# Preparing the experts' first weights in halves of 512 columns, with GpSimd's share behind each head's scaling

## What is computed

```python
x = x + attn_a(layernorm(x))   # 16 heads of 64, causal with ALiBi slopes, then w_out and b_out
x = x + ffn(layernorm(x))      # RMS norm times norm_w, gate, top 2 of 8 experts, swiglu
x = x + attn_b(layernorm(x))   # 8 heads of 128, rotary, causal
x = x + ffn(layernorm(x))      # the same weights again

t1 = jnp.einsum('td,efd->tef', flat, mlp1_w) + mlp1_b     # first weights of the experts: W1
act = _swiglu(t1, LIMIT)
y = jnp.einsum('tei,edi->ted', act, mlp2_w) + mlp2_b
```

## Time and profile before

| what | value |
|---|---|
| timed runs, median of 3 | 2192.08 us (2187.16 to 2192.74) |
| span of the profiled execution, which is also all of its own time that the profile gives | 2234.9 us |
| TensorE busy | 2095.9 us, 94% |
| VectorE busy | 1526.6 us, 68% |
| ScalarE busy | 1439.4 us, 64% |
| GpSimd busy | 1306.3 us, 58% |
| granted TensorE clock, mean | 0.984 |

### The profile page before, as it was taken

One profiled execution on the slowest core, in us unless ns is written; L12 is line 12 of the kernel. 1 busy time (PEld: TensorE's weight loads), 2 busy tenths in 40 slices (PEclk: granted clock), 3 DMA queues, 4 the chain that ended last, 5 costly groups with the idle time before them and its releaser, 6 DMA issues.

```text
span 2234.9 us, 38037 instructions
## 1 busy us (share of the span) xinstructions
PE 2095.9 (94%) x11450; PEld 1670.2 (75%) x11450; DVE 1526.6 (68%) x4368; ACT 1439.4 (64%) x3738; POOL 1306.3 (58%) x1458
## 2 busy tenths in 40 slices
PE   7899999999999999798998999999999999888995
PEld 6677777777777777576776788888888888676774
DVE  7868686868686868466666767566675765656567
ACT  5768686868686867443444777667676676734344
POOL 4655464646464655556665546667576665556663
PEclk9999999999999999999999999999999999999998
DMA  4320010101000000523241001001010000523246
GB/s 146 135 107 29 1 30 1 30 1 30 1 30 1 20 1 22 170 92 83 100 164 56 31 18 38 24 26 41 18 39 18 13 20 26 199 70 106 96 143 232
DMA packets 59500, 134.44 MB, mean 60 GB/s; under 512 B 12900, under 2 KB 30852, under 8 KB 58280
## 3 DMA queue, kind: packets, MB, share of 16 engines
q1 hardware_dynamic: 41576, 94.69, 12.3%
q0 software_dynamic: 17728, 37.32, 5.8%
HBM read 83.60 MB, written 48.40 MB: 59 GB/s over the span
## 4 chain that ended last, share of the span: by engine, by line
PE 75%; DVE 7%; ACT 6%; issue 5%; another core or an unknown queue 3%; DMA 2%; POOL 2%; SPq 0%; ACTq 0%; DVEq 0%; POOLq 0%
PE bank L650 5%; PE bank L1533 5%; PE bank L1553 5%; PE bank L2245 5%; PE bank L672 5%; PE bank L632 4%; PE bank L617 3%; PE bank L2218 3%; PE bank L1518 3%; PE bank L1433 3%; PE bank L618 3%; PE bank L1435 2%; PE bank L1434 2%; PE bank L2220 2%
## 5 line engine op out<-in xcount | busy, mean ns | idle before, releaser
L1157 POOL TENSOR_TENSOR P<-P,rc 128x128 f32<-128x128 f32 (+3 forms) x512 | 354.6, 724 | 351.1 <-DVE rc L964 350.9
L956 DVE CUSTOM_DVE_ANT_0 P<-bank,tab 128x512 f32<-128x512 f32 (+3 forms) x512 | 240.8, 486 | 111.1 <-PE bank L618 107.7
L794 ACT ACTIVATE P<-P,mn 128x128 f32<-128x128 f32 (+3 forms) x512 | 281.6, 552 | 31.1 <-DVE mn L956 26.7
L805 ACT COPY PT<-bank 128x512 f32<-128x512 f32 (+1 forms) x384 | 194.3, 516 | 105.2 <-PE bank L632 95.7
L1992 POOL TENSOR_TENSOR rf<-rp 128x512 f32<-128x512 f32 x128 | 163.7, 1279 | 138.4 <-DVE rp L1833 135.9
L1999 POOL TENSOR_TENSOR q<-rf,q 128x512 fp32r<-128x512 f32 x128 | 162.8, 1293 | 130.9 <-ACT q L1649 130.5
L2493 POOL DMA_INDIRECT yD<-Yf,place x142 | 144.3, 1016 | 148.5 <-ACT Yf L2316 122.2
L632 PE MATMUL bank<-cst,P 128*128 128x128 f32 x1280 | 207.2, 277 | 15.5 <-POOL P L1157 9.7
L617 PE MATMUL bank<-q 128*128 128x512 f32 (+3 forms) x512 | 185.0, 372 | 16.9 <-DVE mn L956 10.8
L632 PEld LDWEIGHTS bank<-cst,P 128*128 128x128 f32 x1280 | 153.1, 141 | 43.7 <-POOL P L1157 13.2
L324 POOL DMA_INDIRECT Gf<-hD,idx x142 | 147.1, 1036 | 59.3 <-issue 38.3
(11 more groups left out here) (257 smaller groups left out, 5913.7 us busy)
## 6 DMA issues: line engine op xcount, KB each, us to landing
hD<-hh SPq DMA_DIRECT2D x16, 512.0 KB
yg<-yD SPq DMA_DIRECT2D x14, 512.0 KB, 4.2
X<-in_x SPq DMA_DIRECT2D x8, 512.0 KB, 4.3
stage<-in_w SPq DMA_DIRECT2D x8, 512.0 KB, 3.5
w1hD<-W1A SPq DMA_DIRECT2D x8, 512.0 KB
w1lD<-stage SPq DMA_DIRECT2D x8, 512.0 KB
rD<-xn SPq DMA_DIRECT2D x8, 512.0 KB
W1lf<-w1lD SPq DMA_DIRECT2D x1, 4096.0 KB
```

What stands on the lines that cost most here:

```text
L794: i = e.activation(ps, ps, ACT.Exp, bias=mn[:, pb, t:t + 1], scale=-1.0, accum_out=rs[:, pb, t:t + 1])
L805: e.copy(PT[:, h % 2, PTO[cs[0]]:PTO[cs[0]] + w], bank[4 + n % 2][:, 0:w]).then_inc(q.a_pt, 1)
L956: e.tensor_tensor_reduce(out=P[:, pb, OFF[t]:OFF[t] + w], in0=score(h, t), in1=tab[:, 512 - w:512], scale=-SLOPES[h % 16], scalar=3e38, op ...
L1157: i = e.tensor_tensor(ps, ps, rc[:, h % 3, t:t + 1].broadcast_to([128, w]), ALU.mult)
```

## The change

W1 is prepared in 16 halves j = 2i + kc of 512 columns. Each half has its own place (stage[:, kc]) and its own semaphores d_w1s[kc] and d_w1o[kc]; the row w0 of expert i goes into one of two places of share, by i % 2. VectorE does norm_w1(u, 0) in the first half of unit u and norm_w1(u, 1) in the second. GpSimd does split_w1(2u-1) between scale(2u+1) and scale(2u+2), and split_w1(2u) at the end of unit u; the last half falls into unit 8. SyncE issues the first two loads together and afterwards load_w1(j+1) behind the stores of half j; stores are 256 KB. The diff, without the declaration of the semaphores:

```diff
@@ -817,7 +818,8 @@
                         if kc == 0 and bt:
                             e.wait_ge(q.m_lg, bt)
                         if kc == 0 and bt == 0:
-                            e.wait_ge(d_w1o, 32 * E)
+                            for s in d_w1o:
+                                e.wait_ge(s, 32 * E)
                         e.copy(hT[:, kc], bank[7][:]).then_inc(q.a_hT, 1)
                     def ratio(bt):
@@ -989,8 +991,9 @@
                                         ALU.subtract).then_inc(v_gw, 1)
                     def norm_w1(i, kc):
-                        e.wait_ge(d_w1s, 32 * i + 32)
-                        e.scalar_tensor_tensor(stage[:, kc], stage[:, kc], nw[:, kc:kc + 1], share[:, 0:512], ALU.mult,
+                        e.wait_ge(d_w1s[kc], (32, 16)[kc] * (i + 1))
+                        w0 = share[:, 512 * (i % 2):512 * (i % 2) + 512]
+                        e.scalar_tensor_tensor(stage[:, kc], stage[:, kc], nw[:, kc:kc + 1], w0, ALU.mult,
                                                ALU.subtract).then_inc(v_w1, 1)
@@ -1102,9 +1105,8 @@
                                 low(u + 2, hl)
                                 if hl:
                                     copy_k(u + 2)
-                            if bt == 0 and hl:
-                                norm_w1(p, 0)
-                                norm_w1(p, 1)
+                            if bt == 0:
+                                norm_w1(p, hl)
                             if v_tile(bt, p, hl):
                                 v_copy(*v_tile(bt, p, hl))
                             if p == 0 and bt:
@@ -1140,12 +1142,12 @@
                                         ALU.mult).then_inc(p_qs, 1)
-                    def split_w1(i):
-                        k = W1_ORDER[i]
-                        raw, H = stage[:].rearrange("p a b -> p (a b)"), W1h[:, k % W1_STAY]
-                        e.wait_ge(v_w1, 2 * i + 2)
+                    def split_w1(j):
+                        i, kc = divmod(j, 2)
+                        raw, H = stage[:, kc], W1h[:, W1_ORDER[i] % W1_STAY, 512 * kc:512 * kc + 512]
+                        e.wait_ge(v_w1, j + 1)
                         e.tensor_copy(H, raw).then_inc(p_w1, 1)
-                        e.wait_ge(p_w1, 2 * i + 1)
+                        e.wait_ge(p_w1, 2 * j + 1)
                         e.tensor_tensor(raw.bitcast(F32R), raw, H.bitcast(F32), ALU.subtract).then_inc(p_w1, 1)
@@ -1193,6 +1195,8 @@
                     for u in range(NU):
                         bt, p = divmod(u, 8)
                         scale(2 * u + 1)
+                        if 0 < u <= E:
+                            split_w1(2 * u - 1)
                         if u == NU - 1:
                             for a in range(4):
                                 gather(e, 0, q, a)
@@ -1210,7 +1214,7 @@
                         if 1 < p < 6 and bt + 1 < NB:
                             add_bias(bt + 1, p - 2)
                         if bt == 0:
-                            split_w1(u)
+                            split_w1(2 * u)
                         if p == 7 and bt and bt + 1 < NB:
                             for n in range(4 if bt == K1 else 2):
@@ -1275,23 +1279,35 @@
                             fetch_x(bt + 2)
                         if bt == 0:
                             e.wait_ge(d_b1, 48)
-                            for i, k in enumerate(W1_ORDER):
+                            def load_w1(j):
+                                i, kc = divmod(j, 2)
                                 if i:
-                                    e.wait_ge(d_w1o, 32 * i)
-                                e.dma_start(stage[:].rearrange("p a b -> p (a b)"), T["w1"][:, k]).then_inc(d_w1s, 16)
-                                e.dma_start(share[:, 0:512], w0D[k].partition_broadcast(128)).then_inc(d_w1s, 16)
-                                e.wait_ge(p_w1, 2 * i + 1)
-                                e.dma_start(w1hD[:, k], W1h[:, k % W1_STAY].bitcast(F32)).then_inc(d_w1o, 16)
-                                e.wait_ge(p_w1, 2 * i + 2)
-                                e.dma_start(w1lD[:, k], stage[:].rearrange("p a b -> p (a b)")).then_inc(d_w1o, 16)
-
-                            e.wait_ge(d_w1o, 32 * E)
+                                    e.wait_ge(d_w1o[kc], 32 * i)
+                                if kc == 0:
+                                    e.dma_start(share[:, 512 * (i % 2):512 * (i % 2) + 512],
+                                                w0D[W1_ORDER[i]].partition_broadcast(128)).then_inc(d_w1s[0], 16)
+                                e.dma_start(stage[:, kc], T["w1"][:, W1_ORDER[i], 512 * kc:512 * kc + 512]).then_inc(d_w1s[kc], 16)
+
+                            load_w1(0)
+                            load_w1(1)
+                            for j in range(2 * E):
+                                i, kc = divmod(j, 2)
+                                k, cs = W1_ORDER[i], slice(512 * kc, 512 * kc + 512)
+                                e.wait_ge(p_w1, 2 * j + 1)
+                                e.dma_start(w1hD[:, k, cs], W1h[:, k % W1_STAY, cs].bitcast(F32)).then_inc(d_w1o[kc], 16)
+                                e.wait_ge(p_w1, 2 * j + 2)
+                                e.dma_start(w1lD[:, k, cs], stage[:, kc]).then_inc(d_w1o[kc], 16)
+                                if j and j + 1 < 2 * E:
+                                    load_w1(j + 1)
+
+                            for s in d_w1o:
+                                e.wait_ge(s, 32 * E)
                             first = [bD[i:i + 1, 0:E * 512].rearrange("a (k n) -> a k n", k=E) for i in range(2)]
-                            e.dma_start(W1A[0:1, 0:W1_STAY, 0].bitcast(F32), first[0][:, 0:W1_STAY]).then_inc(d_w1o, 16)
-                            e.dma_start(w1hD[0:1, :, 0:512], first[0]).then_inc(d_w1o, 16)
-                            e.dma_start(w1lD[0:1, :, 0:512], first[1]).then_inc(d_w1o, 16)
-
-                    e.wait_ge(d_w1o, 32 * E + 48)
+                            e.dma_start(W1A[0:1, 0:W1_STAY, 0].bitcast(F32), first[0][:, 0:W1_STAY]).then_inc(d_w1o[0], 16)
+                            e.dma_start(w1hD[0:1, :, 0:512], first[0]).then_inc(d_w1o[0], 16)
+                            e.dma_start(w1lD[0:1, :, 0:512], first[1]).then_inc(d_w1o[0], 16)
+
+                    e.wait_ge(d_w1o[0], 32 * E + 48)
                     e.wait_ge(q.m_qk, 2 * NU)
                     e.wait_ge(q.m_v, 64)
                     return store, None
@@ -2203,7 +2219,7 @@
                         k, o = a % 2, up_bank(a)
                         if a == 0:
                             e.wait_ge(r_et, 2 * ph + 1)
-                            e.wait_ge(p_w1, 2 * E)
+                            e.wait_ge(p_w1, 4 * E)
                             e.wait_ge(d_w, (32, 208)[ph])
                         if a == L1:
                             e.wait_ge(r_et, 2 * ph + 2)
```

More of the change, by code:

```diff
@@ L155, in program @@
         d_wo = sem("d_wo")
-        d_w1s, p_w1, d_w1o, d_w, d_w2 = (sem(n) for n in ("d_w1s", "p_w1", "d_w1o", "d_w", "d_w2"))
+        p_w1, d_w, d_w2 = (sem(n) for n in ("p_w1", "d_w", "d_w2"))
+        d_w1s, d_w1o = ([sem(f"{n}{kc}") for kc in range(2)] for n in ("d_w1s", "d_w1o"))
         r_ms, r_rk, r_op, r_sl, r_c = (sem(n) for n in ("r_ms", "r_rk", "r_op", "r_sl", "r_c"))
```

## The result

The changed kernel takes 2262.86 us, the median of four runs (2261.53 to 2270.56), against 2189.62 us before (four runs, 2184.23 to 2192.74). The ratio is 1.0334, with a 95% interval of 1.031 to 1.0358: slower by 73.2 us, or 68 to 78. The forecast was 2245.3 us, with a range of 2228 to 2266.

The account below looks back on a forecast made before the run. TensorE sets the pace in the first sentence, with small holes. Load 2 lands at 62.8, 135.7 us later load 15 at 198.5; scores at 200.6 instead of 147.38 add 53.2: 2192.1 + 53.2 = 2245.3 us, range 2228 to 2266.

Parts of the forecast that it names:

- a circle: First sentence, each W1 half: load, norm, minima, reciprocal, scale, split, next load; 6.23 us a step before loads; chance 0.86.
- load of an even half: SyncE issues share, then stage: 3.8 us from the split's end to landing, bounds 2.7 and 5.3.
- load of an odd half: SyncE loads 256 KB of stage alone: 3.0 us from the split's end, bounds 2.2 and 3.9.
- end of split 1: GpSimd's split behind the scaling, before the first late load, load 2: predicted to end at 59.0 us.
- everything else, 13 steps: Non-load work from load 2 to load 15: 81.0 us of steps, plus V copies 5.1, add_bias 3.0, weight subtractions 1.29, deviation 1.5.
- share's 3.4 us: Landing time assumed for the w0 row's load into share, taken as ending the even halves' wait.
- slower splits: GpSimd's half splits, put at 1.87 us each; up to 0.27 x 14 = 4 us more in the upper bound.
- Rival A: TensorE's clock falls to half while it waits in the W1 stretch: at most 16 us more, 2261; chance 0.08.
- Rival B: Loads come in time: half for the whole gain, 2184.9 us, half for one mostly spent, near 2192; chance 0.06.
- The 7.2 us: TensorE's transposes waiting for GpSimd's scaling in five places of the first sentence; reordering by itself would remove up to this.
- Rival C: Same circle with both loads at their lower bounds: 13 us less, 2232; its chance is within the mechanism's 0.86.
- What was costed at nothing: Split 15 in unit 8, 16 more DMA issues on SyncE, W1 stores ending some 4 us later: 0 us.

Follow-up runs that it names:

- refill: Changed kernel, but behind half j's stores the same place is loaded again with half j+2, share issued ahead of the wait for the stores: 2198.6 us, ratio 1.0026.
- split_back: Changed kernel with the odd halves' split returned to the end of the unit before, behind the even half's split: 2232.2 us, ratio 1.0193.
- whole_moved: Kernel before, whole experts and its own loads, with only split_w1(u-1) moved behind scale(2u+1) on GpSimd: 2208.1 us, ratio 1.0077.
- warm16: Changed kernel with 16 useless 128x128 matmuls before the 256-wide scores of heads 8 to 17: 2261.9 us, ratio 1.0326.
- no_loads: Changed kernel without 14 of 16 W1 loads and 7 of 8 w0 loads, so its weights are wrong: 2190.2 us, ratio 0.9993.
- prefetch: Changed kernel with raw weights loaded two experts ahead into W1A, where norm_w1 reads them: 2190.3 us, ratio 0.9999.
- share_early: Changed kernel with the next expert's row w0 loaded one half earlier, behind the odd half's stage load: 2250.8 us, ratio 1.0259.

## Why the prediction was right, and where its size was off

**The direction and the mechanism: right, and shown.** The order on SyncE loads one place at a time, so each half closes a circle through load, norm, reciprocal, scaling and split. The chain shows it link by link, refill takes the loss away by changing that order alone, and split_back and whole_moved move it by taking a scaling out of a circle and putting one in.

**The size: the terms for the loads were too small.** Between the split's end and norm:

| term | predicted | measured | over the stretch |
|---|---|---|---|
| load of an even half, 7 times | 3.8 | 5.27 (4.79 to 5.64) | +10.3 us |
| load of an odd half, 7 times | 3.0 | 3.58 (3.13 to 4.79) | +4.0 us |
| end of split 1 | 59.0 | 60.3 | +1.3 us |
| everything else, 13 steps | | | +1.0 us |

Together 16.7 us: norm of half 15 stands at 215.18 where 198.5 was predicted for its load. The forecast's steps of 10.4 us were 11.5. The term that was mis-sized most is the latency of the even halves. I had taken share's 3.4 us as what ends the wait, on the ground that less is issued ahead of it, and let stage's own 256 KB go unseen behind it. Share did land in 3.7 us in the median (3.3 to 4.2). But stage is issued 0.47 us later and lands 3.9 to 4.8 us after that. With nothing before it but a store, 256 KB of stage landed in 2.7 to 2.8 us in five of seven loads, near the 2.6 of the sum; the other two, halves 5 and 15, took 4.38 and 3.55, and why is open. The even halves lie at my upper bound, 5.3 us; one, 5.64, is clearly above it. That the total stayed inside the range owes something to luck: its top, 2266, also had 4 us for slower splits, which did not come (from 81.99 to 83.92 us a split took 1.93, where 1.87 was put); without them the top would be 2262, and 2262.86 was measured.

By the Trainium skill ("DMA: Bandwidth & Descriptors", "Anatomy of one DMA", a fit for GpSimd's path), 256 KB take an estimated 2.6 us. Five of the seven loads with no share ahead, issued by SyncE, are near it (2.7 to 2.8 us from the issue), and none behind share is.

**Rival A, the clock: wrong.** It fell as described (0.81 in the stretch, 0.50 in a window such as 90 to 94 us), but of the 13 steps only one, from half 12 to half 13, has TensorE in the chain (182.6 to 191.7 us, with 0.50 granted from 182 to 188), and there its work ends together with norm 13 (191.72). So TensorE's work between two landings just has room at half clock too. warm16, which raised the clock to 0.89, took 0.9 us off, which is within the spread of its runs; a run at full clock throughout was not made.

**Rival B, the gain: its price was too high.** The 7.2 us were to be had only on the list of waits. In no_loads and prefetch, where the loads do come in time, the transposes no longer wait for GpSimd, and the stretch ends 3 to 4 us earlier and not 7.2. TensorE then waits 7 to 8 us for VectorE's minima, against 4.8 in the kernel before over the same 36 to 240 us, and all its waits there fall from 16.3 us to 10.9 and 10.3, by less than 7.2: the next engine in line was nearly as late. The times of these runs, near 2190, are what the prediction's second half of this rival had, a gain mostly spent.

**Rival C, quicker transfers: wrong.** The loads were slower than the sum had them and not at their lower bounds: 5.27 and 3.58 us against 2.7 and 2.2.

**What was costed at nothing** held: GpSimd's last half in unit 8, the added issues on SyncE and the later end of the stores left the marker at 69.96, where TensorE's stretch by the same anchors as predicted moved by 69.9, to 217.31 from the 147.38 of the earlier trace rows:

```profile
217.31 0.39 PE L618 MATMUL bank<-q 128*128 128x256 f32 x1 [2.83 <-DVE mn L958]
```

## What to carry to other kernels

Two places are double buffering only if the load for the second is issued before the work on the first has ended; look at what stands ahead of the load on the issuing queue, not at how many places there are. When a task is moved behind another on an engine, follow what it releases all the way round: if the load that it frees feeds a wait ahead of that other task, the latency enters once per turn, and halving the pieces doubles the turns. A preparation loop whose time round is as long as the loop that covers it (12.2 us in 12.6 here) is the first thing to check before touching any part of it.

## What the runs showed of the hardware

**A load behind a broadcast is slow.** 256 KB of stage landed 3.9 to 4.8 us after its issue when share, 256 KB read from one row for all partitions, was issued just ahead of it, and in five of seven cases 2.7 to 2.8 us when it was not. Moving share away in share_early took 2 us from each such load, and the loads that then had share behind them took 0.5 us more on average. Why the broadcast holds up its neighbours was not tried; nor was why two loads with nothing ahead but a store took 4.4 us (the one at 97.59) and 3.6 (211.60).

**VectorE is slower beside GpSimd's cast and subtraction.** When norm_w1 no longer waits for its load, it falls together with GpSimd's work. The tile stage in prefetch:

```profile
L999 DVE SCALAR_TENSOR_TENSOR stage<-W1A,nw,hh x16: 750/962/1670, 42.9 to 139.4; 128x512 f32<-128x512 f32 x16
...
L1154 POOL TENSOR_TENSOR stage<-stage,W1A x16: 1282/1595/1637, 51.0 to 146.9; 128x512 fp32r<-128x512 f32 x16
```

and two of its norms, the first while GpSimd does nothing (81.22 to 83.37 us), the second while it subtracts (126.37 to 127.72):

```profile
81.53 0.75 DVE L999 SCALAR_TENSOR_TENSOR stage<-W1A,nw,hh 128x512 f32<-128x512 f32 x1
...
126.60 1.67 DVE L999 SCALAR_TENSOR_TENSOR stage<-W1A,nw,hh 128x512 f32<-128x512 f32 x1
```

The same norm took 744 to 753 ns in the kernel before and 750 to 753 in the changed one, where VectorE and GpSimd took turns. Here its median is 962 ns: 0.96 to 0.98 us where it begins during GpSimd's cast, 1.53 and 1.67 where it begins early in the subtraction; GpSimd's subtraction has a median of 1595 instead of 1297 ns. Copies of K in pairs took 0.88 us in the kernel before at this place, and 1.19 to 2.32 us in prefetch from 60 to 130 us, beside GpSimd's addition of the bias, cast or subtraction; in the changed kernel too they took 1.31 to 2.05, but ahead of a wait, so it cost nothing there. Beside the scaling of P they were hardly slower (0.92 us at 156.75 in prefetch). That it is the overlap, and not the other source of norm in this kernel, is shown by the two lines above and by no_loads, in which norm reads stage as before and takes 0.93 to 1.66 us in the overlapped halves and 0.75 in the others. Work that is overlapped on these two engines is not free; how much of the reordering's gain this took was not measured.
